# Transposing the probabilities in row halves of the matmul array

## The reference

```python
scores = einsum('bhsd,bhtd->bhst', q, k) / sqrt(64) + causal
probs = softmax(scores)
out = einsum('bhst,bhtd->bhsd', probs, v)
```

## Time and profile before

| what | us |
|---|---|
| median of 3 runs | 303.01 |
| the runs | 302.92 to 303.16 |
| the profiled execution, whole | 303.29 |
| its span, first to last instruction | 301.5 |
| PE busy | 289.6 |
| PEld busy | 235.0 |
| ACT busy | 239.3 |
| DVE busy | 229.7 |
| POOL busy | 213.5 |

### The profile page before, as it was taken

How to read it: one execution, slowest core, us unless ns; L and a number is a source line. 1 busy time by engine, 2 the same in 40 slices (tenths; PEclk the granted TensorE clock), 3 DMA queues, 4 the chain that set the end, 5 groups by cost and what they waited for, 6 DMA issues and landing times.

```text
span 301.5 us, 8603 instructions
## 1 busy us (share of the span) xinstructions
PE 289.6 (96%) x2362; PEld 235.0 (78%) x2362; DVE 229.7 (76%) x909; ACT 239.3 (79%) x863; POOL 213.5 (71%) x325
## 2 busy tenths in 40 slices
PE   8798999999999999999999989999999999999994
PEld 2576888888888888777776779999977778887663
DVE  4889998987777898988898723444377889898981
ACT  4278789898887889989998676677787898999971
POOL 2478878697778669999999982333226899998730
PEclk9999999999999999999999999999999999999999
DMA  6864685879333233444333382000234243543410
GB/s 192 249 133 115 114 276 148 205 194 300 87 75 68 60 75 83 107 101 102 90 97 90 112 245 55 2 0 2 66 93 108 64 113 99 121 106 109 113 37 17
DMA packets 39596, 33.35 MB, mean 111 GB/s; under 512 B 4801, under 2 KB 36674, under 8 KB 39554
## 3 DMA queue, kind: packets, MB, share of 16 engines
q1 hardware_dynamic: 38098, 30.51, 39.8%
q0 software_dynamic: 1024, 2.10, 2.4%
q10 hardware_dynamic: 432, 0.23, 0.3%
HBM read 11.07 MB, written 4.98 MB: 53 GB/s over the span
## 4 chain that ended last, share of the span: by engine, by line
PE 64%; POOL 14%; DVE 9%; issue 6%; DMA 3%; ACT 1%; POOLq 0%; SPq 0%; DVEq 0%; ACTq 0%
PE bank L1199 9%; PE bank L1187 9%; PE bank L1216 8%; PE bank L1450 7%; PE bank L1438 6%; PE bank L1233 6%; POOL probs L499 5%; POOL staged L488 5%; PE bank L1161 3%; DVE rot_out L617 3%; PE bank L1218 3%; PE bank L1189 3%; POOL xn L515 3%; DMA qk_sb<-staged 3%; DVE masked L633 2%
## 5 line engine op out<-in xcount | busy, mean ns | idle before, releaser
L975 ACT ACTIVATE pexp<-masked,negmax 128x128 f32<-128x128 f32 (+1 forms) x256 | 113.9, 452 | 2.2 <-DVE negmax L633 2.2
L499 POOL TENSOR_SCALAR probs<-pexp,rden 128x128 f32<-128x128 f32 (+1 forms) x195 | 84.3, 447 | 27.0 <-DVE rden L640 25.2
L633 DVE CUSTOM_DVE_ANT_0 masked<-bank,mask 128x128 f32<-128x128 f32 (+1 forms) x256 | 75.9, 352 | 21.4 <-PE bank L1189 20.5
L488 POOL TENSOR_TENSOR staged<-rot_out 128x512 f32<-128x512 f32 x56 | 71.4, 1278 | 16.2 <-DVE rot_out L617 15.6
L617 DVE TENSOR_TENSOR rot_out<-bank,rot 128x1024 f32<-128x1024 f32 x64 | 77.7, 1215 | 4.6 <-PE bank L1163 3.5
L997 ACT COPY probsT<-bank 128x384 f32<-128x384 f32 x126 | 54.0, 480 | 27.3 <-PE bank L1199 26.0
L1199 PE MATMUL bank<-ident,probs 128*128 128x128 f32 x384 | 54.0, 275 | 0.7 <-issue 0.5
L975 ACT ACTIVATION_READ_ACCUMULATOR pexp<-masked,negmax 128x1 f32 x256 | 50.0, 195 | 0.0
L1187 PE MATMUL bank<-qk_sb 64*128 64x256 f32 x256 | 47.0, 428 | 1.7 <-DMA qk_sb<-staged 1.3
L1199 PEld LDWEIGHTS bank<-ident,probs 128*128 128x128 f32 x384 | 43.0, 140 | 3.4 <-issue 1.2
L1233 PE MATMUL bank<-vo_sb,ctxT 128*128 128x128 f32 x256 | 37.8, 278 | 0.7 <-ACT ctxT L1004 0.7
(11 more groups left out here) (117 smaller groups left out, 483.6 us busy)
## 6 DMA issues: line engine op xcount, KB each, us to landing
qk_sb<-staged SPq DMA_DIRECT2D x128, 128.0 KB
w_sb<-in_w SPq DMA_DIRECT2D x2, 1024.0 KB, 5.8
w_sb<-in_w SPq DMA_DIRECT2D x4, 512.0 KB, 5.3
sorted_x<-z SPq DMA_DIRECT2D x1, 1408.0 KB, 8.0
sorted_g<-z SPq DMA_DIRECT2D x1, 1152.0 KB, 5.5
out<-res SPq DMA_DIRECT2D x8, 128.0 KB, 2.3
x_sb<-in_x SPq DMA_DIRECT2D x3, 256.0 KB, 3.8
rot<-in_c_rot SPq DMA_DIRECT2D x1, 512.0 KB, 5.7
```

The costliest lines, as they stand in the source:

```text
L488: pool.tensor_tensor(staged[:, n % 2, :, m % 2, :], rot_out[:, m % 2, :, 0:S], rot_out[:, m % 2, :, S:2 * S], op=ALU.add).then_inc(staged_ ...
L499: pool.tensor_scalar(probs[:, g % 2, i, c], pexp[:, g % 2, i, c], rden[:, g % 2, i, k:k + 1], 1.0, ALU.mult, ALU.mult).then_inc(probs_read ...
L633: t = dve.tensor_tensor_reduce(masked[:, g % 2, i, c], s_bank[i][:, c], mask[:, c], -1.0, -NEG * 1e8, ALU.add, ALU.min, negmax[:, g % 2, i ...
L975: e = act.activation(pexp[:, g % 2, i, c], masked[:, g % 2, i, c], ACT.Exp, bias=negmax[:, g % 2, i, k:k + 1], scale=-1.0, accum_out=rowsu ...
```

## The change

`turn` transposes each tile in two halves: queries 0 to 63 of the tile through rows 0 to 63 of the array, queries 64 to 127 through rows 64 to 127, each against the matching 64 x 64 block of the identity. The lower half goes to `t_bank[0]` and the upper half to `t_bank[1]`. So a bank now holds one half of each of the six tiles (64 columns each), of both heads. There are twelve transpositions in place of six.

The copies take over the layout: each copies one bank, 384 columns as before, to the places of its half in `probsT`, which is unchanged (`turned_half`: six runs of 64 columns with a step of 128). Both copies now wait for all twelve transpositions (`probsT_done` at 2g+2), and `turn(g)` waits for both copies of the pair before (`probsT_ready` at 2g) ahead of its first transposition.

```diff
+        def turned_half(g, i):
+            whole = probsT[:, g % 4].rearrange("p i (k q c) -> p (i k) q c", q=2, c=HD)
+            return whole[:, :, i, :]
...
             def late_turned():
                 dve.wait_ge(probsT_ready, 2 * LATE)
+                dve.wait_ge(probsT_done, 2 * LATE + 2)
                 for i in range(2):
-                    dve.wait_ge(probsT_done, 2 * LATE + i + 1)
-                    dve.tensor_copy(probsT[:, LATE % 4, i, :], t_bank[i][:, 0:SW]).then_inc(probsT_ready, 1)
+                    dve.tensor_copy(turned_half(LATE, i),
+                                    t_bank[i][:, 0:SW].rearrange("p (n c) -> p n c", c=HD)).then_inc(probsT_ready, 1)
...
+                act.wait_ge(probsT_done, 2 * g + 2)
                 for i in range(2):
-                    act.wait_ge(probsT_done, 2 * g + i + 1)
-                    act.copy(probsT[:, g % 4, i, :], t_bank[i][:, 0:SW]).then_inc(probsT_ready, 1)
+                    act.copy(turned_half(g, i), t_bank[i][:, 0:SW].rearrange("p (n c) -> p n c", c=HD)).then_inc(probsT_ready, 1)
...
             def turn(g):
+                wait(pe, probsT_ready, 2 * g)
                 for i in range(2):
-                    wait(pe, probsT_ready, 2 * g + i - 1)
                     for k in range(3):
                         if k < 2:
                             pe.wait_ge(probs_ready[i][k], g + 1)
-                        t = pe.transpose(t_bank[i][:, k * P:(k + 1) * P], probs[:, g % 2, i, k * P:(k + 1) * P], ident[:])
+                        for o, r in zip(t_bank, half_rows):
+                            t = pe.transpose(o[:, (3 * i + k) * HD:(3 * i + k + 1) * HD],
+                                             probs[r, g % 2, i, k * P:(k + 1) * P], ident[r, r])
                     t.then_inc(probsT_done, 1)
```

## The result

| | before | after |
|---|---|---|
| median of the timed runs on one chip, us | 302.97 (302.43 to 303.73, 6 runs) | 306.56 (305.99 to 307.83, 6 runs) |
| the profiled execution, whole | 303.29 | 306.38 |
| its span | 301.5 | 304.6 |

The ratio is 1.0127 [1.0098, 1.0156] (in brackets always the 95% interval): 1.3% slower. The prediction of 303.2 missed it by 3.4 us. The time lies inside the range of 301.3 to 307, but outside the likeliest case's own 302.4 to 303.9.

What follows compares the result with a forecast made beforehand. TensorE was taken to bound the slots, TensorE and then POOL the periods. Terms +1.2 - 0.1 - 0.3 - 0.2 - 0.2 - 0.2 = +0.2 us on the profiled 303.29 gave 303.5, by the median 303.2; range 301.3 to 307.

Steps and rivals of the forecast that it cites:

- The twelve halves: Inside `turn` on TensorE: six pairs of halves take five pitches, 0.305 us in place of 0.545, -0.24 us.
- P: Pitch at which the six pairs of halves in `turn` start: taken as 0.061 us, bounds 0.055 to 0.11 or 0.122.
- A: Rival: loads in halves not short or not overlapping, pitch 0.11, each turn 0.25 us more, 314.7; chance 0.18 with D.
- D: Rival: TensorE pairs nothing, halves run in turn, pitch 0.122, 317 us; chance 0.18 together with A.
- The changes of tiling: At the edges of `turn`: +0.04 us between full-array groups, -0.22 behind scores; raw TensorE sum -2.6 us.
- The slots, exposed: TensorE-bound slots, g = 2 to 40: 30 turns at 0.04, +1.2 us; about eight disappear in DMA waits.
- turn(41) and turn(42): Turns after the slots: `turn(41)` on a TensorE chain, -0.3 us; `turn(42)` waits for POOL's scale, -0.2.
- The periods, hidden: Periods: TensorE would save 1.3 us, but POOL's one piece of work covers it, leaving -0.2 us.
- The waits and copies: ACT's copies behind `turn`: first copy some 0.15 us later, inside ACT's waits of 0.65; copy costed at nothing.
- The last slots: Tail, `turn(59)` to 62: savings mostly held by waits for scales and DVE's copy, -0.2 us.
- C: Rival: POOL isn't the bound of the periods, 1.1 us there and 0.4 in the tail gained, 301.7; chance 0.22.
- B: Rival: pitch 0.07, or ACT's delay reaches the next scale; +0.05 us for some 40 turns, 305.2; chance 0.20.

Runs made afterwards that it cites:

- kernel 6: Kernel before, tiles whole, plus one extra 64-row transposition of the identity ahead of `turn` in 38 slots: 314.77 us, ratio 1.0387.
- kernel 2: Kernel before with halves only in the slots, g = 2 to 40: 305.04 us, ratio 1.0077.
- kernel 11: Changed kernel with whole tiles and the old waits for g = 2 to 40: 303.15 us against 303.19 for the kernel before, ratio 1.0005.
- kernel 1: Kernel before with halves only near scores (g = 42, even ones from 44 to 56, and 58 to 61): 302.67 us, ratio 1.0017.
- kernel 5: Kernel before, tiles whole; ACT's first copy waits for all six transpositions for even g from 44 to 56: 305.18 us, ratio 1.0072.
- kernel 3: Kernel before, tiles whole, with only the changed waits: both copies for the sixth transposition, `turn` for both copies: 305.51 us, ratio 1.01.
- kernel 9: Kernel before with halves only for the odd turns of the periods (43 to 55), in place: 302.94 us, ratio 1.0007.
- kernel 8: Kernel before with near-scores halves, plus halves for g = 2 to 39 with `turn` moved right behind scores: 301.7 us, ratio 0.9964.

## Why the prediction was right and wrong

- **The twelve halves: right.** P was taken as 0.061 and is 0.062 by the single records. They pair, so rivals A (0.11) and D (0.122) have fallen. The Trainium skill's rule of columns over 1.2 GHz ("TensorE: Matmul & The Clock Gate", "LDWEIGHTS (loading the stationary operand)"), by which the time would have been about A's, does not hold for these loads.
- **The changes of tiling: right in sum, two terms of it wrong.** +0.04 was predicted for the full array on both sides, +0.05 measured. That they agree is in part luck. The second pair is late behind the change, 0.11 in place of 0.06, which the prediction left out though it has the same for other groups; and the gap behind the halves is 0.15 in place of 0.205. The two cancel. -0.22 behind scores was measured as -0.25. That changing the mode drains the array stands in the Trainium skill ("TensorEngine Tiling (Array Packing)", "Tiling Modes"), without a price; the trace agrees, with 0.04 to 0.1 us of later start each way and a late second load. A change in and out by itself costs 0.31 us in kernel 6.
- **The slots, exposed: the place was right, the sum too small.** It priced 30 turns at 0.04, +1.2 us. The turns themselves fit that: +0.94 up to slot 32 here, and 0.91 over all slots in kernel 2. But the slots cost more than their turns. Profile against profile it is 2.6 us (kernel 11), and two costs stand beside the turns. One is the new waits for queries and keys, 0.69 and 0.44 us, which the prediction had only as cover that absorbs; its own cover at 164.84 is in no other profile, kernels with unchanged slots have new waits of 0.40 to 0.81, and kernel 6 paid nine tenths of its delay, so such a wait is neither a safe cover nor safely the change's doing. The other is the late gather in the tail, 2.1 us, which kernel 2 has in half of its runs. Both are landings of DMAs, and the prediction has no term for them. Why a small delay of the slots moves a gather by more than itself is open: POOL's work stands ahead of them, and POOL's scales are released by the same slots, but no run here took one of them away.
- **turn(41) and turn(42): not settled.** From `scores(41)` to `scores(43)` the changed kernel gains 0.34 us on the one before, but kernels 1 and 5, with `turn(41)` whole, gain 0.33 and 0.26 there too. In the time nothing shows (the six single turns).
- **The periods, hidden: right in size, wrong in the cover.** -0.2 was predicted, and kernel 1 shows none at the end. The cover was said to be POOL, whose work would be one piece. In kernel 1 the periods do get shorter, by 0.5 us in all, until DVE meets a gather that hasn't landed; then POOL itself stands idle for 0.81 us, and one period takes 0.7 us more. Within a period it is ACT's loop from the even copies over the odd ones to `values` that closes it (kernel 5), with next to no slack.
- **The waits and copies: right in the slots, wrong in the periods.** "It arrives early and 0.15 is still inside that" used a mean of 0.65 us over 40 waits. The slots bear it: kernel 3 loses 0.1 us there. In the periods each 0.01 of delay of the even copies would be 0.01 of the period, as kernels 3 and 5 show with 0.33. The changed kernel escapes where halves stand behind scores, because there the sixth pair ends early: in kernel 1 the first copy starts 0.73 us after the last record of the scores, where it was 0.84. In the changed kernel it is 0.74 at `turn(50)` and `turn(52)`, but 0.99 and 1.14 at `turn(48)` and `turn(54)`, and why is open. For the odd turns it is released 0.18 later, and free (kernel 9). Of this step's bounds for the broken run, the zero was right: a copy takes 482 ns, 480 before.
- **The last slots: not settled.** -0.2 was predicted; the changed trace gains 0.2 from `scores(57)` to the last one. Against it stands the low clock in three of six runs, which the prediction doesn't have: these three took 306.74 to 307.83 us, the others 305.99 to 306.38.
- **The rivals.** C's time didn't come, though its ground, that POOL isn't the only cover of the periods, was right. B, nearest with 305.2, put the pitch at 0.07, and it is 0.062. Its second half, ACT's delay reaching the next scale, is to be seen but costs nothing that shows: DVE's reciprocals wait 2.6 us for exponentials from 20 to 172 us, 0.4 before, and in kernel 3, which loses nothing in the slots, it is 3.8. So that the time lies in the range, near B, is luck: the likeliest case is 3.4 us off, and the costs that make up the difference, late DMAs and the clock, are in none of the cases.

The copies of the kernel after, by source line:

```profile
L1003 ACT COPY probsT<-bank x126: 455/482/497, 24.6 to 298.0; 128x384 f32<-128x384 f32 x126
```

## What to carry to other kernels

Price the edges of a group on TensorE and not only its inside: twelve halves saved 0.2 us of transposing and paid more for two changes of tiling; the same halves, with their turns moved next to groups that split the array the same way, gave 1.2%. Don't take a wait for a DMA in one profile as a fixed cover, nor as a fixed cost: look whether it is there in the profiles of other kernels with the same code at this place. A mean wait (0.65 us in 40 cases) is no slack: take it at each place, and follow the loop that comes back to the waiting engine, since idle time inside a closed loop hides nothing. And a stage that gets shorter meets its transfers earlier: ask which of them will not have landed.

## What the runs showed of the hardware

- Pairs of fp32 transpositions through 64 rows each, with 128 columns of weights, start 0.062 us apart, as single ones through 8 rows do (0.061); the second pair behind a change of tiling starts 0.11 us after the first. Whole tiles start 0.109 apart, with the same 128 columns of weights.
- A copy that ACT scatters into six runs of 64 columns costs what a contiguous one costs (482 against 480 ns).
- The granted clock fell to its lower level, 1.2 GHz, for 3.4 us in the tail of two profiled executions. Busy time by stretch in kernel 1 (304.14 us for this execution, against a median of 302.67):

```profile
274.00:280.50 6.50, 5.95 (x58) 4.53 (x58) 5.59 (x25) 6.12 (x26) 6.03 (x8) 1.00 0.48 130
280.50:284.00 3.50, 3.50 (x18) 1.78 (x16) 1.97 (x5) 2.55 (x11) 2.40 (x4) 0.51 0.60 181
284.00:300.00 16.00, 13.98 (x130) 10.20 (x126) 10.44 (x45) 9.77 (x34) 4.05 (x8) 1.00 0.06 16
```

  Ahead of it TensorE had waited several times for scales, and had a record open for 5.95 of 6.5 us. It worked off 18 matmuls in 3.5 us, 58 in 6.5 before. In kernel 8, all turns behind scores, such a fall lies at 277.8 to 281.2. In kernel 1 the runs with a mean clock of 0.992 took 304.14 to 304.69, all others but one 302.07 to 302.73. The changed kernel's own profile has none before its last 2.3 us, so it is no part of the 3.1 us found there.
